# Flamingo gated block on one Trainium2 core: other places and steps for the first expert's weights in the last batch, and the token casts apart

## The chip, the cores and the metric

The kernel runs on one core of one Trainium2 chip. The metric is the device time of one execution in microseconds (us). The core has a matrix engine (TensorE, PE in the profile, with its weight loads as PEld), VectorE (DVE), ScalarE (ACT), GpSimd (POOL) and SyncE (SP), which here only issues DMAs. The engines run their own instruction lists in order and meet at semaphores.

## The reference

The block is a gated cross-attention with a sigmoid in place of the softmax, and then eight experts of a feed-forward net. All is float32.

```python
# x: (16, 224, 512)   ctx: (16, 750, 512)   16 heads of 32
q = (layernorm(x) @ Wq.T) * 32 ** -0.5 ; k = ctx @ Wk.T ; v = ctx @ Wv.T
o = einsum(sigmoid(einsum(q, k)), v) @ Wo.T
x = x + tanh(g_xattn[0]) * o
tokens = layernorm(x).reshape(8, 448, 512)          # two batches per expert
h = gelu(einsum('etd,edf->etf', tokens, w1) + b1)   # w1: (8, 512, 2048)
y = einsum('etf,efd->etd', h, w2) + b2              # w2: (8, 2048, 512)
x = x + tanh(g_ffn[0]) * y
```

## The kernel before, in words

Every product is made to float32 accuracy from three float32r products: an operand is cast to a high part by ScalarE, VectorE subtracts that from the raw value to give a low part, and TensorE adds high x high, high x low and low x high. Each weight or activation therefore passes ScalarE and then VectorE before TensorE may use it.

**Attention.** Python unrolls `body(b, ...)` for b = -1 to 16 (`B`) on every engine. Body -1 prepares batch 0, body 16 ends batch 15. A body has twelve steps. In each step TensorE runs the scores of one step (`scores`, L652: 8 matmuls for four heads), ScalarE turns them into probabilities (`sigmoid`, L837), and TensorE does "fills" beside it: projections of K, V, Q for this or the next batch (`fill`, L620), in an order that the tables `FILL`, `FILL_0` and `FILL_LAST` write out. The scores of a step wait for the sigmoid of the step before, because there is one set of four PSUM banks (`scores_ps`) for them. At step 6, and at step 0 of the next body, `heads` (L669, 48 matmuls, of which the trace holds two records each) multiplies the probabilities of six steps with V. The projected K goes out to a DRAM buffer (`store_k`, POOL, L566) and comes back rearranged, as three DMAs per step that SP issues two steps ahead (`gather_k`, L358); Q goes the same way (`gather_q`). SP's list is in order: what stands behind a DMA whose semaphore is not there yet waits too.

**Sums for the layernorms.** `square` (ScalarE, L887) and `fold` (VectorE, six instructions, L1045 to L1056) write sums of a batch; their scratch is `fold_in(b)`: `q_stage`, and for the last one `x_raw`. POOL stores the sums (`part_scr`), SP loads them back (`load_sums`, `gath`), VectorE's `moments` makes mean and factor from them, and SP's `load_mr` loads those for the next layernorm. `x_res` holds the residual, loaded by `load_residual`.

**Experts.** The hidden layer is in eight chunks of 256 features (`C` = 8). `hidden(e, c, k)` makes 128 features of chunk c (24 matmuls for both k, each k in two halves of 6, L780), `gelu` (L980) and `split_hidden` (L1198, L1200) turn them into operands, and `y(e, c)` adds their product with w2 (24 matmuls, L798). w1 and w2 chunks come by `load_w1` and `load_w2` (L469, L477), and `e_hi` (L964, L967) and `e_lo` (L1187) cast and subtract them. Where a raw chunk lands is set by `raw_of`; the chunks of w1 after the second, and all of w2, land in `v_sb` or `probs`, which the attention uses until its last `heads` (`s_av` at 12 x 16). `xt_hi` and `xt_lo` cast the first expert's 448 tokens, in two halves.

**The seam.** The table `HIDDEN_AT` puts half tiles of the first expert's chunk 0 in steps 7 to 10 of the last batch, in place of fills, and chunk 1, k = 0, behind the last `heads` (entry 12). Then follow the last output projection ("O" tiles), `hidden(0, 1, 1)`, `hidden(0, 2, 0)` and `hidden(0, 2, 1)`, and with `expert(0)` the products `y(0, 0)`, `y(0, 1)` and the loop over the other chunks.

## Time and profile before

| What | Value |
|---|---|
| Time, median of 3 runs | 1693.45 us (1690.64 to 1695.2) |
| The profiled execution's own time | 1685.1 us |
| Its span, first to last instruction | 1683.4 us |
| PE busy | 1667.0 us, 99% of the span |
| PEld, DVE, ACT, POOL busy | 90%, 45%, 47%, 13% |
| TensorE clock granted, mean over the span | 1.000 of full speed |
| DMA | 309.19 MB, mean 184 GB/s |
| Share of the chain that ended last | PE 96%, DVE 2%, DMA 1%, ACT 1% |

The page's time slices show PE nine tenths busy or more in all but the first of forty. Attention takes the time to about 1057 us, the experts the rest. A row with "[0.63 <-ACT probs L837]" tells that the engine stood idle for 0.63 us before it, until an ACT instruction of line 837 released it. A row's duration is from the start of its first instruction to the end of its last, and since matmuls overlap, the next row may begin before that end.

### The profile page before, as it was taken

Reading aid. Unit: us, or ns where it says so; the run is one execution under the profiler, and the core shown is the slowest. Engines: PE = TensorE matmul, PEld = TensorE weight load, DVE = VectorE, ACT = ScalarE, POOL = GpSimd, SP = SyncE. Lnnn points to the kernel's source line nnn. Section 1 sums busy time; section 2 is a strip of 40 time slices with the busy share of each in tenths; the row PEclk is TensorE's granted clock in tenths of the full one; section 3 lists DMA queues with packets and bytes.
Section 4 is the critical chain, followed back from the end, with each engine's and each line's share of the span. In section 5 each row is a group of like instructions: output and inputs, shape, how many; then the busy total and the mean of one; then the engine's idle time right before and its main releaser. Section 6 shows DMA issues by size and latency. Waiting matters only on the chain.

```text
span 1683.4 us, 32954 instructions
## 1 busy us (share of the span) xinstructions
PE 1667.0 (99%) x12763; PEld 1509.8 (90%) x12763; DVE 753.4 (45%) x1290; ACT 787.1 (47%) x956; POOL 219.4 (13%) x323
## 2 busy tenths in 40 slices
PE   8999999999999999999999999999999999999999
PEld 7898898898898898898898888899999999999998
DVE  6343433433433334334334234464646465555554
ACT  5655555555555555555555455333333333334332
POOL 2122122122122122122122121000000000000000
PEclk9999999999999999999999999999999999999999
DMA  7887677686686776777677785446253543526251
GB/s 253 225 227 202 193 224 201 187 237 190 188 238 183 201 228 189 201 221 196 195 221 198 199 227 157 158 135 204 103 184 124 177 141 134 179 97 203 103 169 55
DMA packets 197686, 309.19 MB, mean 184 GB/s; under 512 B 28081, under 2 KB 155601, under 8 KB 197553
## 3 DMA queue, kind: packets, MB, share of 16 engines
q1 hardware_dynamic: 173632, 229.43, 48.4%
q0 software_dynamic: 23920, 77.95, 13.1%
q8 instruction: 89, 1.46, 0.4%
q14 instruction: 45, 0.36, 0.1%
HBM read 228.44 MB, written 78.84 MB: 183 GB/s over the span
## 4 chain that ended last, share of the span: by engine, by line
PE 96%; DVE 2%; DMA 1%; ACT 1%; issue 0%; SPq 0%; ACTq 0%; DVEq 0%; POOLq 0%
PE fill_ps L620 41%; PE scores_ps L798 18%; PE fill_ps L780 13%; PE scores_ps L652 10%; PE heads_ps L669 9%; PE heads_ps L780 4%; ACT probs L837 0%; DMA probs<-WKT_in 0%; PE scores_ps L620 0%; DMA part_scr<-part 0%; DMA k_st<-k_scr 0%; DMA v_sb<-w_in 0%; DVE wV L1187 0%; DVE wQ L1011 0%; DVE wK L1187 0%
## 5 line engine op out<-in xcount | busy, mean ns | idle before, releaser
L837 ACT ACTIVATE probs<-scores_ps 125x1792 f32<-125x1792 f32 x192 | 320.4, 1669 | 139.2 <-PE scores_ps L652 111.0
L798 PE MATMUL scores_ps<-ctx_hl,wK 128*128 128x448 f32 x1536 | 316.6, 362 | 0.0
L798 PEld LDWEIGHTS scores_ps<-ctx_hl,wK 128*128 128x128 f32 x1536 | 288.1, 188 | 19.8
L620 PE MATMUL fill_ps<-ctx_hl,wK 128*128 128x250 f32 x2304 | 298.2, 281 | 1.0 <-DVE wK L1011 0.6
L620 PEld LDWEIGHTS fill_ps<-ctx_hl,wK 128*128 128x128 f32 x2304 | 279.9, 189 | 7.8 <-issue 6.1
L620 PE MATMUL fill_ps<-wV,ctx_hl 128*125 128x512 f32 x1152 | 280.8, 394 | 0.0
L620 PEld LDWEIGHTS fill_ps<-wV,ctx_hl 128*125 128x125 f32 x1152 | 207.8, 185 | 46.3 <-DVE q_stage L1118 0.2
L780 PE MATMUL fill_ps<-wQ,wV 128*128 128x448 f32 x1152 | 243.6, 366 | 3.0 <-DVE wV L1187 3.0
L780 PEld LDWEIGHTS fill_ps<-wQ,wV 128*128 128x128 f32 x1152 | 215.8, 188 | 20.9 <-DVE wV L1187 3.7
L566 POOL DMA_DIRECT2D k_scr<-k_stage x192 | 139.4, 726 | 665.7 <-DVE k_stage L1115 509.3
L652 PEld LDWEIGHTS scores_ps<-q_st,k_st 96*125 96x125 f32 x1536 | 189.1, 188 | 19.4 <-issue 7.7
L652 PE MATMUL scores_ps<-q_st,k_st 96*125 96x224 f32 x1536 | 200.2, 273 | 5.2 <-DMA k_st<-k_scr 2.9
L1115 DVE TENSOR_TENSOR k_stage<-fill_ps,k_stage 128x250 fp32r<-128x250 f32 x192 | 79.9, 417 | 258.7 <-ACT k_stage L861 258.7
L669 PE MATMUL heads_ps<-probs,v_sb 125*32 125x224 f32 x3072 | 151.9, 353 | 0.0
L669 PEld LDWEIGHTS heads_ps<-probs,v_sb 125*32 125x32 f32 x3072 | 96.6, 110 | 45.3
L893 ACT COPY v_sb<-fill_ps 125x512 f32<-125x512 f32 x96 | 56.3, 586 | 165.8 <-PE fill_ps L620 165.8
L980 ACT ACTIVATE q_stage<-fill_ps,b_sb 128x448 f32<-128x448 f32 x96 | 60.8, 635 | 145.5 <-PE fill_ps L780 142.3
L1198 DVE CAST ctx_hl<-q_stage 128x896 fp32r<-128x896 f32 x64 | 40.1, 627 | 159.3 <-ACT q_stage L980 159.3
L1005 DVE TENSOR_TENSOR ctx_hl<-ctx_raw,ctx_hl 128x1000 fp32r<-128x1000 f32 x48 | 57.6, 1200 | 106.1 <-ACT ctx_hl L823 106.1
L620 PE MATMUL fill_ps<-xnT,wQ 128*128 128x224 f32 x768 | 93.6, 274 | 1.4 <-DVE k_stage L1115 1.2
L620 PEld LDWEIGHTS fill_ps<-xnT,wQ 128*128 128x128 f32 x768 | 89.8, 191 | 1.9 <-DVE k_stage L1115 1.4
L861 ACT CAST k_stage<-fill_ps 128x250 fp32r<-128x250 f32 x192 | 69.8, 363 | 42.4 <-PE fill_ps L620 42.3
(98 smaller groups left out, 1347.5 us busy)
## 6 DMA issues: line engine op xcount, KB each, us to landing
k_st<-k_scr SPq DMA_DIRECT2D x576, 125.0 KB, 3.4
v_sb<-w_in SPq DMA_DIRECT2D x94, 512.0 KB, 4.5
k_scr<-k_stage POOLq DMA_DIRECT2D x192, 250.0 KB, 3.9
ctx_raw<-ctxT_in SPq DMA_DIRECT2D x48, 500.0 KB, 4.6
q_st<-q_scr SPq DMA_DIRECT2D x192, 112.0 KB, 3.3
probs<-w_in SPq DMA_DIRECT2D x32, 512.0 KB, 3.8
q_scr<-q_stage POOLq DMA_DIRECT2D x64, 224.0 KB, 4.2
x_res<-xT_in SPq DMA_DIRECT2D x16, 448.0 KB, 4.8
```

The costliest lines, as they stand in the source:

```text
L566: pool.dma_start(scr["k"][j % RING].rearrange("h p s -> p h s"), k_stage[:, j % 3].bitcast(F32)).then_inc(s_k_st[j % RING], 16)
L620: last = pe.matmul(out_, lhsT(kt, a), rhs(kt, c), start=(kt == 0 and t == 0), stop=(kt == KT - 1 and t == 2))
L652: last = pe.matmul(scores_ps[0:ST, j, t * L:(t + 1) * L], k_st3[:, r, j, t * ST:(t + 1) * ST], q_st3[:, slot, j, :], start=True, stop=True)
L669: last = pe.matmul(heads_ps[j * HD:(j + 1) * HD, cols], v_sb[0:ST, v_place(par, 2 * pair + t), mt * P + j * HD:mt * P + (j + 1) * HD], pro ...
L780: last = pe.matmul(hid_ps[bank][:, 0:T], w1[:, slot, a, kt, k * P:(k + 1) * P], xt[:, d, kt, :], start=(kt == 0 and t == 0), stop=(kt == K ...
L798: last = pe.matmul(y_ps[:, dt, 0:T], w2[:, slot, a, k, dt * P:(dt + 1) * P], hid_hl[:, slot, d, k, :], start=(c == 0 and k == 0 and t == 0 ...
L837: nc.scalar.activation(probs[0:ST, s % VISIT], scores_ps[0:ST, :, 0:2 * L], ACT.Sigmoid, scale=SCALE).then_inc(s_probs, 1)
L861: nc.scalar.copy(k_stage[:, j % 3, HI, :], ps[:, 0:SC]).then_inc(hi["K"], 1)
L893: nc.scalar.copy(v_sb[0:ST, v_place(1 - par if i < 2 else par, i % 6), :], fill_bank(b, "V", i)[0:ST, :]).then_inc(done["V"], 1)
L980: nc.scalar.activation(hid[:, k, :], hid_ps[2 * (c % 2) + k][:, 0:T], ACT.Gelu_apprx_tanh, bias=b1[:, 2 * c + k:2 * c + k + 1]).then_inc(s ...
L1005: nc.vector.tensor_tensor(ctx_chunk(c, LO), ctx_raw[:, chunk_place(par, c)], ctx_chunk(c, HI).bitcast(F32), ALU.subtract).then_inc(s_ctx_l ...
L1115: nc.vector.tensor_tensor(k_stage[:, j, LO, :], ps[:, 0:SC], k_stage[:, j, HI, :].bitcast(F32), ALU.subtract).then_inc(done["K"], 1)
```

## The change

It touches two places, the first steps of the attention and the seam, and leaves all arithmetic as it is.

**At the start.** The folds of bodies -1 and 0 use `x_res` as scratch in place of `q_stage`. The waits of the Q tiles on the fold go with it. The load of the first sums moves from step 10 of body -1 to step 0 of body 0; the residual of batch 0 is loaded in step 9 rather than 7, after its fold.

**At the seam.** Chunk 2 of w1 lands in `x_raw` and chunk 0 of w2 in `k_stage`, both in the last batch (issued in steps 7 and 10), so that neither waits for the last `heads`. `HIDDEN_AT` puts two halves in steps 8 and 9, so that chunk 1, k = 0, is done by step 10, and chunk 2, k = 0, stands behind the last `heads`. The two token casts stand in steps 3 and 5 rather than both in 3. The casts of the two chunks, the square, the fold and the gelu take other places. w1 chunk 3 is loaded right after the attention ends, the last batch's sums are loaded in chunk 4 and `moments(B)` moves from chunk 3 to chunk 5.

```diff
-    HIDDEN_AT = {7: [(0, 0, 0)], 8: [(0, 0, 1)], 9: [(0, 1, 0)], 10: [(0, 1, 1)], 12: [(1, 0, 0), (1, 0, 1)]}
+    HIDDEN_AT = {7: [(0, 0, 0)], 8: [(0, 0, 1), (0, 1, 0)], 9: [(0, 1, 1), (1, 0, 0)], 10: [(1, 0, 1)],
+                 12: [(2, 0, 0), (2, 0, 1)]}
...
         def raw_of(e, m, c):
-            if known(e, 0) and m == 1 and c < 2:
-                return x_raw[:, 0:HALF] if c == 0 else ctx_raw[:].rearrange("p r s -> p (r s)")[:, 0:HALF]
+            if known(e, 0) and m == 1 and c < 3:
+                return ctx_raw[:].rearrange("p r s -> p (r s)")[:, 0:HALF] if c == 1 else x_raw[:, 0:HALF]
+            if known(e, 0) and m == 2 and c == 0:
+                return k_stage[:].rearrange("p r h s -> p (r h s)")[:, 0:HALF].bitcast(F32)
...
         def fold_in(b):
-            return x_t if known(b, B) else q_flat
+            if known(b, B):
+                return ctx_raw[:, 0, 0:KT * L].rearrange("p (t l) -> p t l", l=L)
+            return x1T if b < 1 else q_flat
...
+                    if known(b, B - 1) and s == 7:
+                        load_w1(0, 2)
+                    if known(b, B - 1) and s == 10:
+                        load_w2(0, 0)
...
-                    if s == {-1: 10, 0: 8}.get(b, 7) and not known(b, B):
+                    if known(b, 0) and s == 0:
+                        load_sums(-1)
+                    if s == (8 if known(b, 0) else 7) and attends(b):
                         load_sums(b)
-                    if s == (11 if known(b, B - 1) else 7) and attends(b):
+                    if s == {0: 9, B - 1: 11}.get(b, 7) and attends(b):
                         load_residual(b)
...
-                if known(e, 0) and c > 1:
+                if known(e, 0) and c > 2:
                     alone(sp, s_av, STEPS * B)
...
-                if known(e, 0):
+                if known(e, 0) and c == 0:
+                    for r in range(RING):
+                        alone(sp, s_k_st[r], 16 * 2 * B)
+                elif known(e, 0):
                     alone(sp, s_av, STEPS * B)
...
                     if known(b, B) and s == 3:
                         hidden(0, 1, 1)
-                        hidden(0, 2, 0)
                         hidden(0, 2, 1)
...
                         if s == 3:
-                            xt_hi(0)
+                            xt_hi(0, (0,))
                         if s == 5:
+                            xt_hi(0, (1,))
                             e_hi(0, 1, 0)
                         if s == 7:
                             e_hi(0, 1, 1)
+                        if s == 10:
+                            e_hi(0, 1, 2)
                         if s == 11:
                             gelu(0, 0)
-                    if known(b, B) and s == 2:
-                        e_hi(0, 1, 2)
-                        e_hi(0, 2, 0)
+                            e_hi(0, 2, 0)
                     if known(b, B) and s == 10:
+                        square(B, 1)
+                        gelu(0, 1)
                         e_hi(0, 2, 1)
-                        gelu(0, 1)
-                        square(B, 1)
```

VectorE's list changes in the same way (`xt_lo` in halves, `e_lo(0, 1, 2)` in step 10, `e_lo(0, 2, 0)` in step 11, the fold of the last batch ahead of the split of chunk 1).

What this moves, at three places. **SP, from step 10 of body -1 to step 2 of body 0.** `k_st<-k_scr` x3 are the K gathers of one step, `gath` the first sums. Before:

```order
L358 DMA k_st<-k_scr 32x4x250 x3
L367 DMA q_st<-q_scr 32x4x224 x3
L426 DMA gath<-part_scr 32x4x28
L358 DMA k_st<-k_scr 32x4x250 x6
L367 DMA q_st<-q_scr 32x4x224 x3
L358 DMA k_st<-k_scr 32x4x250 x3
L350 DMA ctx_raw<-ctxT_in 128x1000
L358 DMA k_st<-k_scr 32x4x250 x3
```

Now:

```order
L364 DMA k_st<-k_scr 32x4x250 x3
L373 DMA q_st<-q_scr 32x4x224 x3
L364 DMA k_st<-k_scr 32x4x250 x6
L373 DMA q_st<-q_scr 32x4x224 x3
L437 DMA gath<-part_scr 32x4x28
L364 DMA k_st<-k_scr 32x4x250 x3
L356 DMA ctx_raw<-ctxT_in 128x1000
L364 DMA k_st<-k_scr 32x4x250 x3
```

The load of the sums now stands behind the K gathers of steps 1 and 2 and the next Q gather, and ahead of step 3's.

**PE, from the scores of step 8 of the last batch to the expert's first y products.** `scores_ps<-q_st,k_st` are scores, `wQ,wV` the hidden products of the first expert, `oT,wO` the output projection. Before:

```order
L652 MATMUL scores_ps<-q_st,k_st 125x224 x8
L780 MATMUL fill_ps<-wQ,wV 128x448 x6
L652 MATMUL scores_ps<-q_st,k_st 125x224 x8
L780 MATMUL fill_ps<-wQ,wV 128x448 x6
L652 MATMUL scores_ps<-q_st,k_st 125x224 x8
L780 MATMUL fill_ps<-wQ,wV 128x448 x6
L652 MATMUL scores_ps<-q_st,k_st 125x224 x8
L669 MATMUL heads_ps<-probs,v_sb 32x224 x48
L780 MATMUL fill_ps<-wQ,wV 128x448 x12
L620 MATMUL scores_ps<-oT,wO 128x224 x48
L780 MATMUL heads_ps<-wQ,wV 128x448 x12
L780 MATMUL fill_ps<-wQ,wV 128x448 x24
```

Now:

```order
L668 MATMUL scores_ps<-q_st,k_st 125x224 x8
L795 MATMUL fill_ps<-wQ,wV 128x448 x12
L668 MATMUL scores_ps<-q_st,k_st 125x224 x8
L795 MATMUL fill_ps<-wQ,wV 128x448 x12
L668 MATMUL scores_ps<-q_st,k_st 125x224 x8
L795 MATMUL fill_ps<-wQ,wV 128x448 x6
L668 MATMUL scores_ps<-q_st,k_st 125x224 x8
L685 MATMUL heads_ps<-probs,v_sb 32x224 x48
L795 MATMUL fill_ps<-wQ,wV 128x448 x12
L636 MATMUL scores_ps<-oT,wO 128x224 x48
L795 MATMUL heads_ps<-wQ,wV 128x448 x12
L795 MATMUL fill_ps<-wQ,wV 128x448 x12
```

Twelve hidden matmuls moved from behind the O tiles to ahead of them, and in their place twelve moved from behind the `heads` into steps 8 and 9.

**ScalarE, from the probabilities of step 8 on.** `wV` casts are w1 chunks, `wK` casts w2 chunks, `oT` the copy of the last `heads`, `q_stage` with `b1_sb` the gelu. Before:

```order
L837 ACTIVATE probs<-scores_ps 125x1792 x4
L980 ACT_TABLE_LOAD
L980 ACTIVATE q_stage<-fill_ps,b1_sb 128x448 x2
L845 CAST oT<-heads_ps 128x448
L964 CAST wV<-v_sb 128x1024
L967 CAST wK<-v_sb 128x1024
L967 CAST wK<-probs 128x1024
L980 ACTIVATE q_stage<-fill_ps,b1_sb 128x448
L980 ACTIVATE q_stage<-heads_ps,b1_sb 128x448
L887 ACTIVATE x_raw<-x_res 128x896
```

Now:

```order
L853 ACTIVATE probs<-scores_ps 125x1792 x3
L978 CAST wV<-x_raw 128x1024
L853 ACTIVATE probs<-scores_ps 125x1792
L994 ACT_TABLE_LOAD
L994 ACTIVATE q_stage<-fill_ps,b1_sb 128x448 x2
L981 CAST wK<-k_stage 128x1024
L861 CAST oT<-heads_ps 128x448
L900 ACTIVATE ctx_raw<-x_res 128x896
L994 ACTIVATE q_stage<-fill_ps,b1_sb 128x448
L994 ACTIVATE q_stage<-heads_ps,b1_sb 128x448
L981 CAST wK<-probs 128x1024
```

The cast of w1 chunk 2 now stands between the probabilities of steps 10 and 11, the cast of w2 chunk 0 ahead of the copy of the `heads`, and the square ahead of the second gelu.

## Rows read from the trace of the kernel before

**Rows 1.** The page, part 1: TensorE's busy time, share, instructions.
```profile
PE 1667.0 (99%) x12763; PEld 1509.8 (90%) x12763; DVE 753.4 (45%) x1290; ACT 787.1 (47%) x956; POOL 219.4 (13%) x323
```

**Rows 2.** Waits of PE: waiting line, who was waited for; total us, times, longest.
```profile
PE fill_ps L780 <- DVE wV L1187: 3.0, 2, 1.8
...
PE scores_ps L652 <- ACT probs L837: 2.2, 4, 0.6
```

**Rows 3.** Timeline 12 to 75, all engines: start, duration, engine, line, names, [idle before].
```profile
25.56 1.45 POOL L566 DMA_DIRECT2D k_scr<-k_stage  x2 [2.45 <-DVE k_stage L1115]
...
36.57 0.30 SPq L426 DMA_DIRECT2D gath<-part_scr  x1
36.80 1.67 ACT L837 ACTIVATE probs<-scores_ps 125x1792 f32<-125x1792 f32 x1
36.97 2.88 SPq L358 DMA_DIRECT2D k_st<-k_scr  x6
...
41.83 1.14 PE L652 MATMUL scores_ps<-q_st,k_st 96*125 96x224 f32 x8 [2.93 <-DMA k_st<-k_scr]
...
59.59 1.03 PE L652 MATMUL scores_ps<-q_st,k_st 96*125 96x224 f32 x8
```

**Rows 4.** DMA view, 22 to 30: POOL's stores, with the median from issue to landing.
```profile
k_scr<-k_stage POOLq DMA_DIRECT2D x3, 250.0 KB, 4.0
```

**Rows 5.** Line 358 alone, 49.3 to 50.7: three gathers' issue, and their landing.
```profile
L358 SPq DMA_DIRECT2D k_st<-k_scr x3: 325/425/432, 49.4 to 50.2; - x3
...
DMA to landing us min/median/max: 5.3/5.3/6.0
```

**Rows 6.** Timeline of PE, 1015 to 1060: the last batch's steps 5, 8, 9 and after.
```profile
1027.83 1.10 PE L652 MATMUL scores_ps<-q_st,k_st 96*125 96x224 f32 x8 [0.37 <-ACT probs L837]
...
1042.55 1.03 PE L652 MATMUL scores_ps<-q_st,k_st 96*125 96x224 f32 x8
1043.42 1.39 PE L780 MATMUL fill_ps<-wQ,wV 128*128 128x448 f32 x6
1045.43 1.10 PE L652 MATMUL scores_ps<-q_st,k_st 96*125 96x224 f32 x8 [0.63 <-ACT probs L837]
...
1057.04 2.74 PE L780 MATMUL fill_ps<-wQ,wV 128*128 128x448 f32 x12
```

**Rows 7.** Timeline 1000 to 1110, all engines: ScalarE and SP in the last visit.
```profile
1024.34 1.79 ACT L952 CAST wQ<-ctx_raw 128x896 fp32r<-128x896 f32 x2
...
1027.48 0.35 SPq L469 DMA_DIRECT2D ctx_raw<-w_in  x1
...
1032.25 1.05 ACT L964 CAST wV<-x_raw 128x1024 fp32r<-128x1024 f32 x1
...
1046.57 1.67 ACT L837 ACTIVATE probs<-scores_ps 125x1792 f32<-125x1792 f32 x1 [1.28 <-PE scores_ps L652]
...
1054.15 1.28 ACT L980 ACT_TABLE_LOAD   x1
1055.45 1.16 ACT L980 ACTIVATE q_stage<-fill_ps,b_sb 128x448 f32<-128x448 f32 x2
```

**Rows 8.** The same timeline, from 1068: PE's resumed work, and VectorE's fold.
```profile
1068.71 5.12 PE L780 MATMUL fill_ps<-wQ,wV 128*128 128x448 f32 x24 [1.13 <-DVE wV L1187]
...
1072.51 0.62 DVE L1045 TENSOR_TENSOR x_raw<-x_raw 128x448 f32<-128x448 f32 x1
...
1073.67 9.78 PE L798 MATMUL scores_ps<-ctx_hl,wK 128*128 128x448 f32 x48
...
1075.29 0.62 DVE L1056 TENSOR_REDUCE part<-x_raw 128x14 f32<-128x448 f32 x1
```

**Rows 9.** Chain of waits from 1079: start, duration, what.
```profile
1079.29 3.62 DMA v_sb<-w_in
...
1084.01 1.24 DVE wV L1187
```

**Rows 10.** Busy time 1100 to 1150: PE, PEld, DVE, ACT, POOL, clock, DMA share, GB/s.
```profile
1100.00:1150.00 50.00, 50.00 (x250) 46.58 (x249) 32.99 (x39) 19.49 (x24) 1.07 (x2) 1.00 0.42 145
```

More of the change, by code:

```diff
@@ L949, in xt_hi @@
                     act.wait_ge(full["Q"], 4 * B)
-                for half in range(2):
+                for half in halves:
                     act.wait_ge(s_normed, 2 * e + half + 1)
@@ L1245, in expert @@
                     split_hidden(e, c)
-                    if first and c == 3:
+                    if first and c == 5:
                         moments(B)
```

50 lines of the change are left out of this document (26 added, 24 removed).

## Prediction

> **What bounds the kernel now.** I read the page first: TensorE is busy for 1667.0 of the span's 1683.4 us [rows 1]. Nothing of its work is removed here (the hidden products only change places), so the change can win or lose only at the 16.4 us in which PE stands. The view of PE's waits says who ends them: VectorE's w1 subtraction (3.0 us in two waits, the longer 1.8) and the sigmoids (2.2 us in four) [rows 2]; one more, of 2.93 us at the very start, ends with a K gather's landing [rows 3]. The timelines then tell what stands ahead of each. A matmul group's successor normally starts some 0.16 us before the group's modelled end (scores at 1042.55 + 1.03 = 1043.58, next group at 1043.42 [rows 6]), so a wait removed gives its printed length and about 0.16 us.
>
> **Term 1, the start: -3.1 us.** PE wants the scores of step 1 at 41.83 - 2.93 = 38.90, and gets them at 41.83 when its K gather has landed. That gather was issued at 36.97, right behind the load of the sums at 36.57 [rows 3]: SP stood at the sums' semaphore with the gather queued behind. The K tile itself had been stored from 25.56 on [rows 3], and such a store lands in 4.0 us [rows 4], so the gather can be issued at about 29.6. Even with the slowest landing that I use here, 6.0 us after the last issue [rows 5], it is there by 37. The other condition is the probabilities of step 0: 36.80 + 1.67 = 38.47, in time. The sums are still loaded when their store is there, so the next layernorm is not earlier or later. The gain lies between 0 and 3.1 us; I take all, since both other conditions are met before 38.90.
>
> What is late next is step 5's gather. SP waits before it for the first means, which nothing speeds up directly: three DMAs from 49.4 to 50.2, landed at the latest at 50.2 + 6.0 = 56.2 [rows 5]. The scores of step 5 start at 59.59 [rows 3] and would want them at 56.5. That is 0.3 us to spare if the DMAs stay as slow, more if the early gathers thin out the traffic. Cost 0, at worst some 1.5 us if the landing is 2 us later.
>
> The scratch of the two folds, the later residual and the missing waits of the Q tiles have one answer: the fold's six instructions are the same, on the same bytes' worth of data, and no PE wait ends at a Q copy; 0.
>
> **Term 2, the token casts apart: -0.5 us.** Both casts (1.79 us) run from 1024.34 [rows 7], ahead of a sigmoid, and the scores of step 5 then wait 0.37 us [rows 6]. With one cast of 0.9 us the sigmoid is 0.9 earlier and the wait goes: 0.37 + 0.16. It can't give more, nor cost here.
>
> The second cast now stands in step 5, ahead of w1 chunk 0's, which ran at 1032.25 [rows 7]. So the tokens are finished at about 1031.75 + 0.9 + 1.05 = 1033.7, and SP's load of w1 chunk 1, which waits for both halves and was issued at 1027.48 [rows 7], goes out 6.3 us later. Behind it on SP stand step 8's K gather, a Q gather and step 9's. Step 8's goes out from 1034.1 to 1035.0 and, with 6.0 us [rows 5], lands by 1041.0; its scores want it at 1042.55 - 0.5 = 1042.05 [rows 6]. Cost 0. The chunk itself lands in 3.62 us [rows 9], by 1037.7, some 4 us before the time of step 7's sigmoid, behind which it is cast.
>
> **Term 3, halves into steps 8 and 9: -1.4 us.** In steps 8 to 10 the beat is ScalarE's: it waits 1.28 us for the scores and takes 1.67 for the sigmoid, 2.95 us a step [rows 7], while PE has 0.87 us of scores (1042.55 to 1043.42) and one half tile, and waits 0.63 [rows 6]. Twenty-four hidden matmuls take 4.96 us (1068.71 to 1073.67 [rows 8]), six 1.24. With two halves a step is 0.87 + 2.48 = 3.35 us, PE's beat. The two steps grow from 2.88 (1042.55 to 1045.43) and 2.95 to 6.70, by 0.9 to 1.0 us with a margin for the changeover, and the 2.48 us behind the `heads` go: -1.4. Ends: 0 if sigmoids come late for another reason, -1.9 if nothing is lost.
>
> The cast of w1 chunk 2 goes between the sigmoids of steps 10 and 11. Such a cast takes 1.05 us and the pause there is 1.28 [rows 7], so it fits. Its load is issued after about 1036; the load of w2 chunk 0 stands behind the last K gather, so no gather waits for either; 0.
>
> **Term 4, the two waits on w1: -3.2 us.** The chunk 2 products stopped for 1.13 us at 1068.71 [rows 8], since their chunk could only land after the attention; now it is ready before the `heads` end. The second wait, 1.8 us [rows 2], follows a load that went out at 1079.29 behind the sums of the last batch: 3.62 us of landing, a cast, 1.24 us of subtraction [rows 9]. That load now goes out when the attention ends, 20 us earlier. Both waits gone give 1.13 + 1.8 and twice the 0.16. Bounds: -3.2 and 0.
>
> **Term 5, a new wait at the O tiles: +0.2 us.** From 1027 on I count in the time of before, and leave term 1 out. The `heads` end at about 1057.04 - 0.5 + 1.1 = 1057.65. ScalarE, 0.6 us later than before too, loads its table from 1054.75, does two gelus to 1057.2 [rows 7], casts w2 chunk 0 until 1058.3, and only then copies the `heads`. VectorE subtracts w2 chunk 0 first (1.24 us [rows 9]), to 1059.5, and the output's low part, 0.62 us like the other operations of that size [rows 8], to 1060.2. PE ends its twelve chunk 2 matmuls at 1057.65 + 2.48 = 1060.1 and waits for it. I put 0.2; the ends are 0 and the 1.5 us of the case below.
>
> The fold (1072.51 to 1075.91, 3.4 us [rows 8]) now precedes the split of chunk 1 and the subtraction that the second y product needs. From the end of the O tiles PE has 24 hidden and 24 y matmuls before it, 4.96 + 4.9 = 9.9 us; the chain is 3.4 and five more operations of at most 1.24, so at most 9.6. Cost 0, thinly. `moments(B)` moves within a stage where VectorE is busy for 33 of 50 us [rows 10]: 0.
>
> **Sum.** -3.1 - 0.5 - 1.4 - 3.2 + 0.2 = -8.0 us. The profiled execution took 1685.1 us, so its like would take 1677.1. It lies 8.35 us below the median of the runs shown, 1693.45, against which the kernel is judged; the sum applied to that gives **1685.4 us**.
>
> **A rule weighed against the rows.** The table load of the gelu stands in the chain of term 5. The rows show 1.28 us for it at 1054.15, and the first gelu at 1055.45, at once behind [rows 7]; the last sigmoid ended at 1046.57 + 2 x 2.95 + 1.67 = 1054.14, so nothing lies before it either. The Trainium skill, page "ScalarE: Activation LUTs", section "What ACT_TABLE_LOAD costs", adds a drain of about 1.38 us to every switch to another set. Here the trace disagrees with it, and I go by the trace.
>
> **Rivals.**
> - **The start is taken back.** Step 5's gather, or the layernorm behind the means, is late for the earlier PE. The 0.3 us to spare speak for it, the idle DMA time before 36 against. Up to 3.1 us are lost: 1685.4 to 1688.5. Chance 0.12.
> - **The last visit is crowded.** Three more weight loads beside the K gathers, and SP held by the tokens, make scores of steps 8 to 11 wait 1 to 2 us: about 1687. Against it stand the landing bounds of term 2. Chance 0.10.
> - **A drained switch.** A pause of 1.4 us at the table load, as one case of ScalarE being late: PE would wait for the gelu 0.4 us and for the output's low part 1.4 in all, 1.2 more than in term 5: 1686.6. The rows of before have no such pause. Chance 0.03.
> - **The seam gives nothing.** Each wait there is replaced by another (the output copy, the second y product), and only the start remains: 1690.3. Chance 0.05.
> - **Slower.** SP is held at w1 chunk 1 by the second token half. From 1037 on, as against the 1033.7 above, each us of holding delays step 8's scores by one, and all behind. It would have to last to 1045 to eat the 8.0 us. The cast has only one copy and a sigmoid ahead of it, so I see no way there. Chance 0.03, at 1696 to 1700.
>
> **How the numbers follow.** My forecast has 0.67. About 0.3% (5.1 us) is what a measurement of this kernel can tell from no change. Faster by more: the forecast, most of the first three rivals: 0.82. Within: the fourth rival, the rest of the first, and a little for the spread of the runs (4.6 us between lowest and highest): 0.14. Slower: 0.04. The range: the best ends of the terms give -8.7, the fourth rival -3.1, that is 1684.8 to 1690.3; a median of a few runs may lie some 2 to 3 us off either way, which I add in full only below. So 1681.5 to 1690.5.
>
> **What would show it.** In the changed profile PE's wait for the gather near 39 is gone, and its load of sums stands behind the gathers; steps 8 and 9 of the last batch take 3.4 us each without an [ACT probs] wait; no wait of PE ends at VectorE's w1 subtraction; PE's idle time falls from 16.4 to about 9; a wait of some tenths may stand at the first O tile. Wrong would be: a wait of scores near 56 or near 1042, a wait of the second y product, or a span that falls by less than 5 us.

## The result and the profile after

The changed kernel takes 1679.45 us (median of ten runs, 1677.88 to 1686.47). The kernel before, in the same comparison, takes 1689.07 us (ten runs, 1684.79 to 1695.2). The ratio is 0.9938, with a 95% interval of 0.992 to 0.9955: faster by 0.45% to 0.8%, or 9.6 us between the medians. The forecast of the change, -8.0 us on 1693.45, is a ratio of 0.9953 and lies in that interval. The forecast of the time, 1685.4, does not hold, and its range (1681.5 to 1690.5) misses the time by 2 us: the median of the kernel before that it started from was 4.4 us higher than that of ten runs.

The profiled execution took 1679.16 us, with a span of 1677.5 (1683.4 before). The head of its page, against [rows 1]:

```profile
span 1677.5 us, 32958 instructions
...
PE 1665.9 (99%) x12763; PEld 1510.0 (90%) x12763; DVE 753.3 (45%) x1290; ACT 787.0 (47%) x956; POOL 219.4 (13%) x323
```

PE's idle time went from 16.4 to 11.6 us. The waits of PE in the changed kernel (waiting line, who was waited for; total us, times, longest), against [rows 2]:

```profile
PE scores_ps L668 <- DMA k_st<-k_scr: 3.3, 3, 1.5
PE heads_ps L764 <- POOL ident L562: 1.7, 1, 1.7
PE fill_ps L636 <- DVE k_stage L1129: 1.6, 2, 1.2
```

The view goes on with waits that the kernel before has too, all before 35 us. Both waits on VectorE's w1 subtraction and all four on the sigmoids are gone. So is the 2.93 us one at the start. New are three waits for K gathers. The first is at step 5 of batch 0. Timeline of the changed kernel, 25 to 60, SP and PE (start, duration, engine, line, names, [idle before]), against [rows 3]:

```profile
29.68 2.70 SPq L364 DMA_DIRECT2D k_st<-k_scr  x6
...
38.66 1.03 PE L668 MATMUL scores_ps<-q_st,k_st 96*125 96x224 f32 x8
...
39.28 0.30 SPq L437 DMA_DIRECT2D gath<-part_scr  x1
...
50.11 0.84 SPq L425 DMA_DIRECT2D x_mr<-stat_scr  x2
...
51.11 2.34 SPq L364 DMA_DIRECT2D k_st<-k_scr  x3
...
57.13 1.13 PE L668 MATMUL scores_ps<-q_st,k_st 96*125 96x224 f32 x8 [0.65 <-DMA k_st<-k_scr]
```

Step 1's gather goes out at 29.68 and its scores start at 38.66, not 41.83. But the sums are loaded at 39.28, where they were at 36.57: 2.7 us later. The means follow, and step 5's scores wait 0.65. The sums are late because their store is. POOL issues it at the same time (33.51, 33.59 before), but it lands later. The store `part_scr<-part` in the kernel before:

```profile
DMA to landing us min/median/max: 2.9/2.9/2.9
```

and in the changed one:

```profile
DMA to landing us min/median/max: 5.7/5.7/5.7
```

The early K gathers of steps 1 and 2 (750 KB, issued 29.68 to 32.38) are in the air beside it. From 32 to 34 us the view of windows gives the DMA engines a share of 1.05; in the kernel before it is 0.02 there.

The other two are in the last batch. The same view, 1024 to 1085, all engines, against [rows 6 to 8]:

```profile
1031.45 0.35 SPq L481 DMA_DIRECT2D ctx_raw<-w_in  x1
...
1036.18 0.37 SPq L481 DMA_DIRECT2D x_raw<-w_in  x1
1037.42 0.72 POOL L582 DMA_DIRECT2D k_scr<-k_stage  x1 [7.48 <-DVE k_stage L1129]
...
1039.59 1.03 PE L668 MATMUL scores_ps<-q_st,k_st 96*125 96x224 f32 x8
...
1042.90 1.03 PE L668 MATMUL scores_ps<-q_st,k_st 96*125 96x224 f32 x8
...
1047.83 1.13 PE L668 MATMUL scores_ps<-q_st,k_st 96*125 96x224 f32 x8 [1.47 <-DMA k_st<-k_scr]
...
1051.35 1.13 PE L668 MATMUL scores_ps<-q_st,k_st 96*125 96x224 f32 x8 [1.17 <-DMA k_st<-k_scr]
...
1054.20 1.28 ACT L994 ACT_TABLE_LOAD   x1
...
1055.50 1.16 ACT L994 ACTIVATE q_stage<-fill_ps,b_sb 128x448 f32<-128x448 f32 x2
...
1057.09 2.70 PE L795 MATMUL fill_ps<-wQ,wV 128*128 128x448 f32 x12
...
1069.87 9.76 PE L814 MATMUL scores_ps<-ctx_hl,wK 128*128 128x448 f32 x48
...
1079.47 2.60 PE L795 MATMUL fill_ps<-wQ,wV 128*128 128x448 f32 x12
```

At step 8 the changed kernel is 2.96 us ahead (39.59 against 42.55). When the `heads` are done it is ahead by nothing (1057.09 against 1057.04). From there to chunk 3 it gains 5.8, since before chunk 3 began here, with its wait on w1:

```profile
1085.29 2.70 PE L780 MATMUL fill_ps<-wQ,wV 128*128 128x448 f32 x12 [1.84 <-DVE wV L1187]
```

That gain is kept to the end (spans 5.9 apart). What lies behind the two gather waits is not the gather's issue but the landing of the K store ahead of it. The issues of `store_k` between 1037 and 1041 in the changed kernel:

```profile
DMA to landing us min/median/max: 4.7/5.7/6.8
```

and between 1040 and 1044 in the kernel before:

```profile
DMA to landing us min/median/max: 3.1/3.2/3.3
```

Two loads of 512 KB (w1 chunk 1 at 1031.45, 4.0 us later than before, and w1 chunk 2 at 1036.18, new here) stand right in front of these stores. Between the two go out the three K gathers, three Q gathers and three K gathers that stand behind chunk 1 in SP's list, 1.1 MB in all, from 1031.96 to 1036.08.

### The profile page after: what moved, and what is told of

It reads as the page before. It is cut to its first block, busy times and chain, and to the rows that moved or that the text cites. A ratio compares the mean times of both kernels' runs of the same rounds, so it can differ in the third digit from the quotient of the medians.

```text
span 1677.5 us, 32958 instructions
## 1 busy us (share of the span) xinstructions
PE 1665.9 (99%) x12763; PEld 1510.0 (90%) x12763; DVE 753.3 (45%) x1290; ACT 787.0 (47%) x956; POOL 219.4 (13%) x323
## 4 chain that ended last, share of the span: by engine, by line
PE 96%; DMA 2%; DVE 1%; SPq 0%; ACT 0%; issue 0%; POOLq 0%; DVEq 0%; ACTq 0%
PE fill_ps L636 40%; PE scores_ps L814 18%; PE fill_ps L795 13%; PE scores_ps L668 10%; PE heads_ps L685 9%; PE heads_ps L795 5%; DMA k_st<-k_scr 1%; DMA k_scr<-k_stage 0%; DMA probs<-WKT_in 0%; DMA part_scr<-part 0%; PE scores_ps L636 0%; DMA stat_scr<-st_row 0%; SPq L364 0%; DMA gath<-part_scr 0%; DVE wQ L1025 0%
```

## The experiments

Each ratio is to the kernel before, run beside it on the same chip in the same comparison; it differs from the ratio of the two medians by up to 0.06%. Its median there was 1688.46 us (23 runs) for the first four, 1688.34 (26) for the next four and 1687.98 (24) for the last four of the table.

| Kernel | Median us (runs) | Ratio, interval | Profiled span |
|---|---|---|---|
| e1, start only | 1684.48 (12) | 0.9977, 0.9965 to 0.9990 | 1683.3 |
| e2, seam only | 1685.88 (12) | 0.9980, 0.9969 to 0.9991 | 1685.7 |
| e3, w1 chunk 2 late | 1677.06 (6) | 0.9934, 0.9916 to 0.9952 | 1677.9 |
| e4, and means late | 1678.83 (6) | 0.9940, 0.9923 to 0.9957 | 1679.5 |
| e5, and sums early | 1679.28 (9) | 0.9946, 0.9930 to 0.9963 | 1677.9 |
| e6, stalls filled | 1685.66 (12) | 0.9985, 0.9972 to 0.9997 | 1684.0 |
| e7, extra load | 1688.96 (10) | 1.0005, 0.9985 to 1.0025 | 1685.1 |
| e8, casts together | 1677.72 (6) | 0.9943, 0.9922 to 0.9965 | 1674.9 |
| e9, changed kernel again | 1679.85 (6) | 0.9947, 0.9933 to 0.9961 | 1681.6 |
| e10, casts together, chunk 2 late | 1678.85 (7) | 0.9950, 0.9931 to 0.9969 | 1675.4 |
| e11, halves at their old steps | 1682.64 (12) | 0.9967, 0.9952 to 0.9981 | 1680.8 |
| e12, kernel before again | 1687.25 (10) | 0.9997, 0.9984 to 1.0011 | 1685.7 |

### Which part brings what: e1 and e2

e1 is the kernel before with the part at the start alone:

```diff
-            return x_t if known(b, B) else q_flat
+            return x_t if known(b, B) else x1T if b < 1 else q_flat
...
-                    if s == {-1: 10, 0: 8}.get(b, 7) and not known(b, B):
+                    if known(b, 0) and s == 0:
+                        load_sums(-1)
+                    if s == (8 if known(b, 0) else 7) and attends(b):
                         load_sums(b)
```

with the waits of the residual and of the Q tiles that go with it. 

> The kernel before with the start part of the change alone (fold scratch, place of the first sums' load, residual of batch 0). My theory: the wait of the scores of step 1 goes (3.1 us) and 0.65 us of it comes back at step 5, whose K gather stands behind a mean load that is now later: span 1683.4 - 2.5 = about 1681, ratio about 0.9985. Rival: the start is where most of the 9.6 us between the medians lies (the profile pair shows only 5.9): ratio 0.997 or lower.

It is faster by 0.23%, 3.9 us of 1688.46 (1.7 to 5.9). Step 1's scores start at 39.59 without a wait, and step 5's wait 0.30 at 57.71. Yet its profiled span is 1683.3: TensorE's granted clock was 0.83 of full between 1080 and 1090, behind the wait on w1 that this kernel keeps. In the first profile of before it was 1.00 there. So 12 and 12 hidden products that took 4.97 us (1085.29 to 1090.26) took 6.53. Another 0.8 us was lost before the change could act: at about 10 us, PE waits for VectorE's first K weights, 0.58 us in the first profile of before and 1.67 here. This wait is in every kernel and goes from none (e3, e16) to 2.36 us (e7) over the eighteen profiles, so two spans can differ by a microsecond or more for it alone. Without both losses the span would be the expected 1681.

e2 is the changed kernel with those same lines turned back. 

> The changed kernel with the start part undone. Theory: between the scores of step 6 of the last batch and the first product of chunk 3 the change gains 5.8 us less what the start put in (2.9 us by step 8 of which 0.5 by the token casts), and the waits for the K gathers of steps 10 and 11 are as long or shorter than 1.5 and 1.2 us: the span falls by 3.0 to 3.5 us if those waits stay (about 1680), ratio 0.998. Rival: the two K gathers wait because of the start part's earlier time alone, not because of the loads: then the seam alone gives 5 us or more.

It is faster by 0.20%, 3.4 us (1.5 to 5.2; the medians differ by 2.6). Terms 2 to 5 made 4.9 of it. Its start, in the timeline of PE:

```profile
41.46 1.58 PE L667 MATMUL scores_ps<-q_st,k_st 96*125 96x224 f32 x8 [2.70 <-DMA k_st<-k_scr]
42.84 4.17 PE L635 MATMUL fill_ps<-ctx_hl,wK 128*128 128x250 f32 x24
```

The 24 fills take 4.17 us here and 2.97 in the first profile of before. The stall was 0.2 us shorter, but this time the clock fell (0.83 in 40 to 50). The hidden products also ran at a slower pace in this profile (see e14 below), which costs 5.4 us. Without that and the 1.6 us that the clock took the span would be about 1678.7, 4.7 below the first profile of before. In the last batch the scores of step 10 wait 1.21 us for their K gather, and the K stores land in 5.2 to 6.4 us. So the late stores don't need the earlier PE that the start part brings: the rival named for e2 falls.

The two parts together make 7.3 us, against 9.6 and 8.9 (e9, 0.53% of 1687.98) for the whole: near enough for their intervals.

### What delays the K stores: e3, e7, e8, e10, e9

e3 is the changed kernel with the load of w1 chunk 2 behind the last K gather:

```diff
-                    if known(b, B - 1) and s == 7:
-                        load_w1(0, 2)
                     if known(b, B - 1) and s == 10:
+                        load_w1(0, 2)
                         load_w2(0, 0)
```

> The changed kernel with the load of w1 chunk 2 issued after the last K gather (step 10) in place of step 7. Theory (the load crowds the DMA engines and the K tiles' stores land after 4.7 to 6.8 us, not 3.2): the stores land in 3.5 us or less, the waits of scores 10 and 11 for their gathers (1.47 and 1.17 us) go, and the span falls by about 2.5 us to 1675. Rival (the chain store, gather, scores is late because PE runs 3 us ahead of it, whatever is loaded): both waits stay within 0.5 us, span 1677 to 1678. If the chunk is then late for its cast, a wait of the products behind the heads shows it.

In the last batch it does what was expected: the stores land in 3.2 us, no gather is waited for, and PE is busy for 19.40 of the 20 us from 1040 to 1060, against 17.36 in the changed kernel. Its span is no shorter, though (1677.9). Step 5 of batch 0 waited longer in this execution, and the clock fell (0.92 in 50 to 60, 0.91 in 60 to 70):

```profile
58.22 1.82 PE L667 MATMUL scores_ps<-q_st,k_st 96*125 96x224 f32 x8 [2.00 <-DMA k_st<-k_scr]
59.84 3.89 PE L635 MATMUL fill_ps<-wV,ctx_hl 128*125 128x512 f32 x12
```

(12 such fills take 2.96 us at that place in the changed kernel.) Nothing that e3 edits lies there, so the wait at step 5 is one that varies between executions: 0.30 in e1, 0.65 in the first profile of the changed kernel, none in e8 and e9, 2.00 here. Even the kernel before has it once (0.36, e13).

Is it the extra load alone? e7 is the kernel before with such a load added at step 7, for data that nobody uses:

```diff
+                    if known(b, B - 1) and s == 7:
+                        alone(sp, s_ew_lo[1], 1)
+                        sp.dma_start(x_raw[:, 0:HALF], io["w1"][bass.ds(0, 1), 2].rearrange("a p f -> p (a f)")).then_inc(s_extra, 16)
```

(ScalarE waits for it before it casts again.) 

> The kernel before with one more 512 KB load, w1 chunk 2 into x_raw, in step 7 of the last batch, as the changed kernel has it; nothing reads it, the last batch's square waits for its landing. Theory (the load itself crowds the K tiles' stores and gathers): the two K stores land in 4 us or more in place of 3.1 to 3.3, and the scores of step 10 wait for the K gather by 0.3 to 1 us; span +0.5 to +1.5. Rival (only the pace of PE matters): landings as before within 0.3 us and no wait for a gather in the last batch.

Not here: the ratio is 1.0005, and no gather is waited for in the last batch. The load went out at 1036.29, the first store at 1042.02, and the stores landed in 3.0 to 3.3 us. The theory that 512 KB more in step 7 of the kernel before crowd the stores falls. But the load led the first store by 5.7 us, and in the changed kernel it leads by 1.2 (1036.18, 1037.42). A lone load as close as that was not run.

e8 is the changed kernel with the token casts together again:

```diff
-                            xt_hi(0, (0,))
-                        if s == 5:
-                            xt_hi(0, (1,))
+                            xt_hi(0)
+                        if s == 5:
```

and VectorE's `xt_lo` likewise. 

> The changed kernel with both token casts in step 3 again. Theory: the scores of step 5 wait 0.37 us again, but w1 chunk 1 is loaded 6 us earlier and out of the way of the K stores, so that the waits of scores 10 and 11 (2.6 us) shrink by 0.5 to 1.5 us: span 1676.5 to 1677.5, no slower than the change. Rival (w1 chunk 2 alone makes them wait): the two waits keep their 2.6 us and the span grows by up to 0.5 us, since the earlier PE is caught at the same gather: 1677.5 to 1678.

Its waits of PE from 35 us on:

```profile
PE scores_ps L668 <- ACT probs L853: 1.0, 2, 0.6
```

and its last batch, with SP and POOL:

```profile
1031.78 0.37 SPq L481 DMA_DIRECT2D x_raw<-w_in  x1
...
1037.07 0.71 POOL L582 DMA_DIRECT2D k_scr<-k_stage  x1 [7.25 <-DVE k_stage L1128]
...
1039.24 1.03 PE L668 MATMUL scores_ps<-q_st,k_st 96*125 96x224 f32 x8
...
1042.55 1.03 PE L668 MATMUL scores_ps<-q_st,k_st 96*125 96x224 f32 x8
...
1045.85 1.03 PE L668 MATMUL scores_ps<-q_st,k_st 96*125 96x224 f32 x8
```

The stores land in 3.0 to 3.4 us, no gather is waited for, and steps 8 and 9 take 3.31 and 3.30 us. The span, 1674.9, is 8.5 us below the first profile of before, of which 0.6 lies before 11 us, where nothing was changed. So two things come together. The cast of the second token half in step 5 holds w1 chunk 1 on SP, and with it the nine gathers behind it; the load of chunk 2 follows them; and all of it goes out in the 6 us before POOL stores K. Taking away either the load (e3) or the hold (e8) is enough for PE to wait for no gather. e8 moves more than chunk 1, though: its gathers end at 1031.67 and chunk 2 goes out at 1031.78, 5.3 us ahead of the first store. Which of these transfers weighs most is therefore not shown. And with the load alone taken away the landing is not always back at 3.2: in e4 and e5, which have the edit of e3, it is 2.8 to 4.4 and 3.9 to 4.4 us.

e10 does both, the edits of e3 and of e8. 

> The changed kernel with both token casts in step 3 and the load of w1 chunk 2 after the last K gather. Each alone took the two waits away, so the second adds nothing: span 1675 to 1676, 0 to 1 us against the casts together alone, and 2 us or more under the changed kernel's own span of this call. Rival: the late chunk is cast late (behind the gelu), which delays the last heads' copy and brings a wait of 0.5 us or more at the O tiles.

Again no gather is waited for (span 1675.4). It gains nothing over e8. ScalarE's cast of chunk 2 now waits 0.70 us for its load, and that reaches PE: the O tiles begin 2.79 us after the first product behind the `heads`, against 2.55 in e8. In e5 the cast waits 1.30 us, and the O tiles wait 0.54 for the output's low part. So the late load has a price of some tenths, as the rival said, and e8's edit one of 0.37 us at step 5 of the last batch. One of the two is enough.

e9 is the changed kernel, unaltered, once more. 

> The changed kernel once more, beside the three others of this call on one chip. Theory: waits of 1 to 3 us in all for K gathers at steps 10 and 11 of the last batch, as in its first profile, and of some tenths at step 5 of batch 0; ratio to before 0.993 to 0.995. Rival: those waits were of that one execution: the second profile has none in the last batch.

The mechanism recurs in a milder form. The stores land in 3.4 to 5.3 us, step 10's scores wait 1.10 instead of 1.47, and step 11's wait for no gather:

```profile
1047.06 1.13 PE L668 MATMUL scores_ps<-q_st,k_st 96*125 96x224 f32 x8 [1.10 <-DMA k_st<-k_scr]
```

The medians of the changed kernel (0.9938 and 0.9947) and of e3, e8 and e10 (0.9934, 0.9943, 0.9950) can't be told apart. The gather waits cost 2.3 us in one profile (from step 8 to the end of the `heads` 17.50 us, against 15.21 in e8), less in the other, and that is below what six runs resolve. By the profiles e8 is the best version; by the medians no version is shown to beat the changed kernel.

### Can the wait of step 5 be mended? e4 and e5

e4 is e3 with the next layernorm's means loaded one step later, behind the gather:

```diff
-                    if s == 2 and known(b, 0):
+                    if s == 3 and known(b, 0):
                         load_mr(1)
```

> As the one before, and in batch 0 the load of the means moves from step 2 to step 3 of SP's list, behind step 5's K gather. Theory: the wait of 0.65 us at the scores of step 5 goes too, span about 1674.5. Rival: the layernorm of batch 1 is then late for its Q tile or for VectorE's K work, which costs as much again: span 1675 to 1677.

The gather is in time (scores of step 5 at 56.51, no wait), and the wait comes back where the layernorm is late:

```profile
63.49 1.61 PE L667 MATMUL scores_ps<-q_st,k_st 96*125 96x224 f32 x8 [3.15 <-ACT probs L852]
```

ScalarE's list has the layernorm's copy ahead of that sigmoid. A wait of SP became a longer one of ScalarE.

e5 is e3 with the sums loaded between the gathers of steps 1 and 2:

```diff
-                    if known(b, 0) and s == 0:
+                    if known(b, -1) and s == 11:
                         load_sums(-1)
```

> The changed kernel with w1 chunk 2 loaded after the last K gather, and the first sums loaded right behind step 1's K gather, ahead of step 2's K gather and the Q gather. Theory: the wait at step 1 stays away, the sums' store lands near 36.5 again, the means are loaded by about 48.5, and step 5's gather is in time: no wait of PE for a K gather in the whole profile, span about 1674.5, ratio to before about 0.992. Rival: step 2's K gather, now issued after the sums, is late for its scores (wanted near 42) by more than 0.5 us, and the sum is no better than 0.9934.

The load goes out 1.3 us sooner (37.99), since the store of the sums, with only three gathers ahead of it, lands in 3.6 us instead of 5.7. But the means are not loaded sooner (51.01 against 50.11), and step 5's scores wait 1.55. POOL stores the means at 44.50, 1.0 us sooner than in the changed kernel, and this store lands in 6.4 us instead of 4.5. Over the eighteen profiles it takes 3.4 to 6.7 us. Both attempts failed.

### Were the half tiles worth their move? e11

e11 is the changed kernel with the old table and `hidden(0, 2, 0)` behind the O tiles:

```diff
-    HIDDEN_AT = {7: [(0, 0, 0)], 8: [(0, 0, 1), (0, 1, 0)], 9: [(0, 1, 1), (1, 0, 0)], 10: [(1, 0, 1)],
-                 12: [(2, 0, 0), (2, 0, 1)]}
+    HIDDEN_AT = {7: [(0, 0, 0)], 8: [(0, 0, 1)], 9: [(0, 1, 0)], 10: [(0, 1, 1)], 12: [(1, 0, 0), (1, 0, 1)]}
...
                         hidden(0, 1, 1)
+                        hidden(0, 2, 0)
                         hidden(0, 2, 1)
```

> The changed kernel with the half tiles of the first expert at their old steps (chunk 1, k = 0, behind the heads), all else as changed. Theory: moving the halves was worth nothing, because the K gathers end steps 10 and 11: the span is that of the changed kernel within 0.6 us, and the waits for the gathers turn into sigmoid waits. Rival: it was worth its 1.4 us all the same: span 1.4 longer.

It is slower than e9, beside it on the same chip, by 2.8 us of median (1682.64 against 1679.85). The intervals, 0.9952 to 0.9981 and 0.9933 to 0.9961, just overlap, so the size is uncertain. Its last batch:

```profile
1048.47 1.14 PE L667 MATMUL scores_ps<-q_st,k_st 96*125 96x224 f32 x8 [3.25 <-DMA k_st<-k_scr]
1049.44 2.20 PE L795 MATMUL fill_ps<-wQ,wV 128*128 128x448 f32 x6
1051.45 1.92 PE L667 MATMUL scores_ps<-q_st,k_st 96*125 96x224 f32 x8
```

With one half tile a step PE stood for 3.25 us in one piece, in place of 1.47 and 1.17 in two. After it the clock fell (0.84 in 1050 to 1060): six hidden matmuls took 2.20 us instead of 1.38. From the scores of step 8 to chunk 3 this profile takes 42.78 us, the first of the changed kernel 39.88. That is 2.9 more, twice the 1.4 us of term 3. The moved halves also split a stall, and what followed the stall in one piece, the slower products, is part of the difference.

### The clock and the spread of the runs: e6, e12 and e13 to e16

e6 shortens nothing. It fills two stalls of the kernel before with matrix transposes of a constant, whose results nobody reads:

```diff
+                    if known(b, 0) and s == 1:
+                        turns(22)
                     if attends(b):
                         scores(b, s)
...
+                    if known(e, 0) and c == 3:
+                        pe.wait_ge(s_gelu, 4)
+                        turns(12)
                     for k in range(2):
```

> The kernel before with PE kept busy inside two of its stalls: 22 transposes of the identity ahead of the scores of step 1 in batch 0, 12 ahead of the products of chunk 3. Theory (in part of the executions the granted clock falls after these stalls, so that a stall costs more than its length): no 10 us stretch has a clock under 0.99 except after the 1.1 us stall near 1068 or at the end, the median falls by 1 to 3 us against before, ratio 0.998 to 0.999, and no wait gets shorter than before in total. Rival (the runs spread only because DMAs land at other times): the same median within 0.3 us, or up to 0.5 us more.

It is faster by 0.15% (0.03 to 0.28), 2.7 us between the medians, and the granted clock is at least 0.99 in every 10 us but the last. So keeping PE at work through a stall buys something by itself, though the interval comes close to none. The mean clock of every run is on record and says the same. Of e6's 12 runs 10 are at 1.000 and none is below 0.999; of the 26 runs of the kernel before beside them 3 are at 1.000 and 17 at 0.998 or less. Over all 88 runs of the kernel before in these experiments the time goes with it: the medians are 1685.9 us at 1.000 (12 runs), 1686.9 at 0.999 (28), 1688.6 at 0.998 (30) and 1690.3 at 0.997 (13).

e12 is the kernel before, unaltered, once more. 

> The kernel before once more, for a second profile of it. Theory: PE waits again for step 1's K gather by 2.5 to 3.5 us, and the granted clock may or may not be below 1.0 in the 10 us after one of its long waits; where it is, the matmuls there take about 1.5 to 2 times as long and the span is 1 to 3 us over 1683. Rival: clock at 1.0 throughout, and a longer span comes with longer waits for DMAs.

Its span is 2.3 us longer than the first profile's. Some 0.5 of it is there before the scores of step 1 start (PE is 0.3 later from the early wait on, and this stall is 0.17 longer), and most of the rest comes right behind them:

```profile
42.32 1.75 PE L652 MATMUL scores_ps<-q_st,k_st 96*125 96x224 f32 x8 [3.10 <-DMA k_st<-k_scr]
43.86 3.99 PE L620 MATMUL fill_ps<-ctx_hl,wK 128*128 128x250 f32 x24
```

Clock alone did not explain runs of the kernel before at 1693 to 1696, nor why e9's profiled execution had a span of 1681.6 with fewer waits and a clock of 1.00. So four single executions of the kernel before were profiled. 

> The kernel before, unchanged, one look. Theory (pace): the highest times of a kernel are executions in which the hidden products of the experts go at 2.48 us for twelve matmuls (2.64 shown) in place of 2.43 (2.60 shown), as in two of the fourteen profiles so far, with the clock at 1.00; that is worth 5.3 us, so a profiled execution above 1690 shows 2.64 all through the experts, and one below 1689 shows 2.60. Rival (clock): an execution above 1690 shows 2.60 with the clock at 1.00 and instead several windows of 10 us at 0.83 to 0.85 beyond the one or two near 40 and 1080.

 

> As the look before, a second draw. Pace: 2.64 if it is above 1690, 2.60 if below 1689. Clock: 2.60 in either case, and more windows at 0.83 to 0.85 the longer it is.

 

> As the look before, a third draw. Pace: 2.64 if it is above 1690, 2.60 if below 1689. Clock: 2.60 in either case, and more windows at 0.83 to 0.85 the longer it is.

 

> As the look before, a fourth draw. Pace: 2.64 if it is above 1690, 2.60 if below 1689. Clock: 2.60 in either case, and more windows at 0.83 to 0.85 the longer it is.

Three (e13, e15, e16) came out at 1686.1, 1685.74 and 1686.41 us, with 2.60 us for twelve hidden matmuls. The fourth, e14, took 1694.8. Its timeline of PE at the start and in the experts:

```profile
41.83 2.02 PE L652 MATMUL scores_ps<-q_st,k_st 96*125 96x224 f32 x8 [2.74 <-DMA k_st<-k_scr]
43.65 4.91 PE L620 MATMUL fill_ps<-ctx_hl,wK 128*128 128x250 f32 x24
...
1088.11 4.16 PE L780 MATMUL fill_ps<-wQ,wV 128*128 128x448 f32 x12 [1.78 <-DVE wV L1187]
...
1109.25 2.64 PE L780 MATMUL fill_ps<-wQ,wV 128*128 128x448 f32 x12
1111.73 2.64 PE L780 MATMUL heads_ps<-wQ,wV 128*128 128x448 f32 x12
1114.21 4.96 PE L798 MATMUL scores_ps<-ctx_hl,wK 128*128 128x448 f32 x24
```

and the windows of the same execution (PE, PEld, DVE, ACT, POOL busy, clock, DMA share, GB/s):

```profile
40.00:50.00 10.00, 8.17 (x44) 8.03 (x45) 3.44 (x18) 2.94 (x4) 1.26 (x2) 0.66 1.07 238
...
1100.00:1650.00 550.00, 550.00 (x2707) 507.36 (x2706) 303.36 (x340) 195.51 (x240) 4.27 (x8) 1.00 0.45 148
```

The same last window in the first profile of before:

```profile
1100.00:1650.00 550.00, 550.00 (x2732) 512.23 (x2731) 305.50 (x335) 197.35 (x242) 4.28 (x8) 1.00 0.45 149
```

Both theories hold at once. At full clock, the hidden products start every 2.48 us per twelve (1109.25, 1111.73, 1114.21), not every 2.43, to the end of the kernel: in 550 us 25 recorded matmuls fewer. The products with w2 are not slower. And the clock fell twice. From 1088.11 to the last block of y products at 1680.29 e14 takes 6.9 us more than before takes (1085.29 to 1670.56), of which some 5.4 are the pace, as e9 shows (from chunk 3 to there 590.57 us, against 585.17 in the first profile of the changed kernel). The rest, and the 2.8 us that it is behind when the `heads` end (1059.84 against 1057.04), lie where the clock fell. That is the 9.7 us between the two spans.

The clock of 0.66 is a mean of two levels. Single microseconds of e14, 43 to 44 and 48 to 49, stand at half and at full clock:

```profile
43.00:44.00 1.00, 1.00 (x7) 1.00 (x6) 0.41 (x3) 0.12 (x1) 0.00 (x0) 0.50 1.15 221
...
48.00:49.00 1.00, 1.00 (x11) 1.00 (x10) 0.01 (x1) 0.37 (x1) 0.65 (x1) 1.00 1.09 169
```

The six profiles of the kernel before have a stall at the same place, PE's wait for step 1's gather. What the clock makes of it:

| | first profile | e12 | e13 | e14 | e15 | e16 |
|---|---|---|---|---|---|---|
| wait, us | 2.93 | 3.10 | 2.88 | 2.74 | 2.77 | 2.84 |
| mean granted clock, 40 to 50 | 1.00 | 0.83 | 1.00 | 0.66 | 1.00 | 0.83 |

Two variants have the same stall: e2 (2.70 us, 0.83) and e7, with the longest of all (3.15 us, 1.00).

## Why the prediction was right and wrong

**The sign and the size of the change: right.** -8.0 us was forecast (0.9953). Measured are 0.9938 (0.992 to 0.9955) and, in e9, 0.9947 (0.9933 to 0.9961).

**The time itself: the step that failed is the last of the sum, "the sum applied to that".** The mechanism and the size of the change were right; the base it was set on was not. The 1693.45 us came from three runs, all at 1690.64 or above. Ten runs with these three among them have a median of 1689.07, and three more comparisons gave 1688.46, 1688.34 and 1687.98. Only 17 of the 88 runs in the experiments are as high as 1690.64, so three out of three was a rare draw, or had a cause that the record doesn't show. The prediction noted that the profiled execution lay 8.35 us below the three, and took both as given. That gap was the sign: e14, an execution of 1694.8 us, differs from the profiled one by a slower pace in the experts, which the change doesn't touch, and by the clock behind two stalls, which it removes. That the three were such executions is argued from their times; none of them was profiled, and their clocks are not on record. The range allowed 2 to 3 us for it, and it was 4.4. On the median of ten the same sum gives 1681.1, 1.6 above the measured.

**Term 1 (-3.1): the gain right, its side effect wrong.** Step 1's scores moved by 3.2 us. "The next layernorm is not earlier or later" was wrong: the sums are loaded 2.7 us later (39.28 against 36.57) and the means 1.7 later (50.11 against 48.40), and step 5's scores wait 0 to 2.0 us, where the prediction put 0 and at worst 1.5. The sums' store lands in 5.7 us instead of 2.9 beside the early gathers (4.6 in e1, 3.6 in e5, where step 2's gathers go out after it has landed). The prediction had noted that the early gathers fall into idle DMA time, but priced no store beside them. By itself the part brought 3.9 us of median.

**Term 2 (-0.5): the gain right; "cost 0" for the 6.3 us later load of w1 chunk 1 wrong.** Step 8's gather was in time, as reckoned. What was not reckoned was that the load and the nine gathers held behind it go out right before POOL stores K, and that with the load of chunk 2 behind them a store lands in up to 6.8 us instead of 3.2. This is the same omission as in term 1.

**Term 3 (-1.4): wrong in the changed kernel, right without the crowding.** "No gather waits for either; 0" failed at 1047.83 and 1051.35. In e8 steps 8 and 9 take 3.31 and 3.30 us against the 3.35 forecast, and the stretch from step 8 to the end of the `heads` grows by 0.72 (15.21 against 14.49), where 0.9 to 1.0 was put. In the changed kernel it is 17.50. This is the rival "the last visit is crowded", given 0.10. It named the right symptom (1 to 2 us in steps 8 to 11), but thought of the gathers; the place is the store ahead of them. Its time, 1687, was reckoned from the same base of 1693.45 and is further off than the forecast. In the profiles the change gains 5.9 us, 2.1 less than the sum. That the medians came out at the forecast size is in part luck, since the clock, which no term had, added to them.

**Term 4 (-3.2): right.** Both w1 waits are gone (1.13 and 1.84 us). From the end of the `heads` to chunk 3 the changed kernel takes 22.38 us against 28.25: 5.9 less, of which the two waits with their changeovers make 3.3 and the twelve matmuls moved ahead 2.4.

**Term 5 (+0.2): 0.** No wait stands at the O tiles or at the second y product, so the thin margins there held. They are thin indeed: in e5, with chunk 2 late, the O tiles wait 0.54.

**The rule on the table load.** The changed kernel repeats what the rows of before showed: the load takes 1.28 us at 1054.20, and the gelu follows at 1055.50. The Trainium skill's extra drain (page "ScalarE: Activation LUTs", section "What ACT_TABLE_LOAD costs") is again not seen.

**What no term had: the clock behind a stall.** The prediction priced a stall at its length and 0.16 us. At the stall at the start the clock fell in three of six executions, and the 24 fills then took 3.84 us (e16), 3.99 (e12) or 4.91 (e14) instead of 2.97, the scores ahead of them up to 0.9 longer. A kernel that has the stall pays that in part of its runs, and medians see it: e6 removes nothing but this and gains some 2.7 us. The profiles of before and after were both at full clock and differ by 5.9 us; the medians differ by 9.6. That the clock makes up most of the rest is what e6 and the clocks of the runs support: 12 of 88 runs of the kernel before are at 1.000, but 9 of 16 of the changed one (its first ten and e9). Their medians there are 1685.9 and 1678.7, so as an estimate 7.3 us are left at like clock. It isn't split off exactly, since the runs come from several comparisons. The Trainium skill, page "TensorE: Matmul & The Clock Gate", section "What's actually happening", has the clock at one of two levels, 1.2 and 2.4 GHz, by how busy the array has been. The rows agree: e14's microseconds from 42 to 47 stand at 0.50 and those from 48 at 1.00, so 0.66 and 0.83 are means over ten us with both; they add that after the same stall it falls in one execution and not in another.

Of the signs named beforehand, the gather wait at 39, the sums behind the gathers, the sigmoid and w1 waits came as said; steps 8 and 9 took 3.31 and 4.93 us, the second with a gather wait in it, where 3.4 was put for each. PE's idle time fell to 11.6, not 9, and two of the signs of being wrong appeared: a wait of scores near 56 (57.13), and others a little behind 1042.

## What to carry to other kernels

Before a sum is set on a median, ask whether the profiled execution belongs to the same population: here the median of three runs lay 4.4 us above that of ten, more than any term of the sum, and only the ratio of a comparison was steady. Price a load that moves later by what it will be in the air beside, stores of other queues too, and not only by who waits for it or stands behind it. And treat a stall of TensorE of some 2 to 3 us as its length plus a chance of a stretch at half clock; splitting such a stall with work that is due anyway can be worth more than the work's own time.

## What the runs showed of the hardware beyond expectation

- **A second pace at full clock.** In three of eighteen profiles (e2, e9, e14) the hidden products of the experts ran with 2.48 us between starts of twelve instead of 2.43, from about the O tiles or chunk 3 to the end, at a granted clock of 1.00. The cost is 5.4 us of some 600. Products with w2 (4.96 us for 24) were not slower. It came in the kernel before, in the changed one and in e2, so it doesn't need the change. Its cause is open.
- **The clock behind a stall is not the same from run to run.** 2.74 us of waiting went with a mean of 0.66 over 40 to 50 us (e14); 2.88, 2.93 and even 3.15 (e13, the first profile, e7) with 1.00. Stalls of 1.78 and 1.91 us before chunk 3 were followed by half clock (e14, e1), others of 1.84 and 1.90 there were not (the first profile, e12).
- **A store's landing depends on what else flies.** `k_scr` stores of 250 KB landed in 3.1 to 3.3 us before, in 4.7 to 6.8 in the changed kernel, in 3.4 to 5.3 in its repetition, in 3.0 to 3.4 with the token casts together (e8), and in 2.8 to 4.4 with chunk 2 late (e3, e4, e5). The small store of the sums took 2.9 before and 5.7 in the changed kernel. The Trainium skill, page "DMA: Bandwidth & Descriptors", section "Latency and other measured facts", gives HBM's access latency as 0.2 us on average and 2 at high load. The direction agrees; the rows show up to 3.6 us more, which that figure alone doesn't cover.
